# Expert outputs scattered by token inside the expert loop and read back with plain loads; the gated unit without its products of resident weights

## The reference

```python
x = x + 0.5 * moe(layernorm(x))      # 8 experts, 2 a token, F=512, layer norms inside
x = x + gated_unit(layernorm(x))     # groups of 64, relu^2 scores, linear part
x = x + 0.5 * moe(layernorm(x))      # the same weights again
x = x + 0.5 * swiglu_moe(layernorm(x))
x = x + attention(layernorm(x))
x = x + 0.5 * swiglu_moe(layernorm(x))
```

```python
probs, idx = top_k(softmax(xt @ Wr + br), 2); probs = probs / probs.sum()
h = layernorm(relu(xt @ W1[e] + b1[e])) * g1[e] + be1[e]
y = layernorm(relu(h @ W2[e] + b2[e])) * g2[e] + be2[e]
out = sum over the two chosen e of probs[e] * y[e]
```

## Time and profile before

| | |
|---|---|
| median of three runs | 2130.17 us (2128.75 to 2130.4) |
| the profiled execution | 2112.62 us, span 2110.8 us |
| mean granted TensorE clock | 0.908 |
| busy: TensorE | 1813.6 us, 86% |
| busy: TensorE weight loads | 1379.7 us, 65% |
| busy: VectorE | 1239.8 us, 59% |
| busy: ScalarE | 689.7 us, 33% |
| busy: GpSimd | 584.9 us, 28% |

### The profile page before, as it was taken

How to read it: one execution, slowest core, us unless ns; L and a number is a source line. 1 busy time by engine, 2 the same in 40 slices (tenths; PEclk the granted TensorE clock), 3 DMA queues, 4 the chain that set the end, 5 groups by cost and what they waited for, 6 DMA issues and landing times.

```text
span 2110.8 us, 38449 instructions
## 1 busy us (share of the span) xinstructions
PE 1813.6 (86%) x10812; PEld 1379.7 (65%) x10813; DVE 1239.8 (59%) x4206; ACT 689.7 (33%) x1279; POOL 584.9 (28%) x946
## 2 busy tenths in 40 slices
PE   3758994899844699299999969999999998999998
PEld 2547992555533699289988955555555555988987
DVE  2555885555545588566666555665655652556654
ACT  0114551222200355122232214444444442232222
POOL 2652675566257366532211010000000000000000
PEclk9758996999855799699999969999999998999999
DMA  5111212000001121100000000000000000000001
GB/s 200 38 43 51 60 50 93 25 20 21 3 29 45 57 60 55 55 21 12 19 11 11 1 0 1 1 0 0 0 0 0 0 0 1 1 0 0 0 1 41
DMA packets 61796, 54.18 MB, mean 26 GB/s; under 512 B 8579, under 2 KB 55044, under 8 KB 61189
## 3 DMA queue, kind: packets, MB, share of 16 engines
q1 hardware_dynamic: 52070, 34.20, 5.3%
q0 software_dynamic: 8192, 16.79, 2.7%
q10 hardware_dynamic: 1440, 2.10, 0.3%
HBM read 31.56 MB, written 21.50 MB: 25 GB/s over the span
## 4 chain that ended last, share of the span: by engine, by line
PE 70%; POOL 10%; DVE 8%; issue 8%; DMA 2%; SPq 1%; POOLq 1%; ACT 1%; DVEq 1%; ACTq 0%
PE bk L1007 14%; PE bk L1664 10%; PE bk L582 6%; PE bk L990 5%; PE bk L992 5%; PE bk L991 5%; POOL xs L368 4%; PE bk L1652 3%; PE bk L575 3%; PE bk L1639 2%; PE bk L1590 2%; PE bk L564 2%; PE bk L565 2%; PE bk L566 2%; DMA sb_X<-x 1%
## 5 line engine op out<-in xcount | busy, mean ns | idle before, releaser
L1007 PEld LDWEIGHTS bk<-sb_wd,sb_sc 128*128 128x128 f32 (+1 forms) x2688 | 333.0, 192 | 23.2 <-DVE sb_X L1106 3.6
L1007 PE MATMUL bk<-sb_wd,sb_sc 128*128 128x128 f32 (+1 forms) x2688 | 336.7, 275 | 0.0
L1092 DVE TENSOR_TENSOR sb_sc<-sb_sb_,bk 128x512 f32<-128x512 f32 x224 | 152.2, 684 | 230.4 <-PE bk L992 220.2
L112 POOL TENSOR_TENSOR sb_ln_ve<-sb_ln_mv,sb_eps 128x2 f32<-128x2 f32 (+1 forms) x48 | 9.4, 195 | 998.9 <-DVE sb_ln_mv L104 998.9
L1046 ACT ACTIVATE sb_sb_<-bk 128x512 f32<-128x512 f32 x224 | 133.8, 598 | 444.8 <-PE bk L992 442.0
L1918 DVE TENSOR_REDUCE sb_sc<-bk 128x2 f32<-128x512 f32 x256 | 164.6, 688 | 157.0 <-PE bk L1639 153.0
L1664 PE MATMUL bk<-sb_sa,sb_sb_ 128*32 128x256 f32 x1024 | 249.1, 387 | 0.7 <-ACT sb_sc L1813 0.7
L1826 ACT ACTIVATE sb_sa<-bk 128x512 f32<-128x512 f32 x256 | 151.1, 597 | 185.0 <-PE bk L1652 184.9
L1106 DVE SCALAR_TENSOR_TENSOR sb_X<-bk,sb_gate,sb_X 128x128 f32 (+1 forms) x576 | 161.4, 342 | 4.2 <-PE bk L1007 1.8
L582 PE MATMUL bk<-sb_w2c,sb_sb_ 128*128 x1152 | 152.2, 275 | 0.0
L368 POOL DMA_INDIRECT xs<-sb_xn,sb_send_row x128 | 128.7, 1006 | 80.3 <-DVE sb_send_row L357 44.0
(11 more groups left out here) (284 smaller groups left out, 3427.4 us busy)
## 6 DMA issues: line engine op xcount, KB each, us to landing
sb_sc<-xs SPq DMA_DIRECT2D x144, 64.0 KB, 1.9
ys<-sb_sc SPq DMA_DIRECT2D x36, 256.0 KB, 2.3
xs<-sb_xn,sb_send_row POOLq DMA_INDIRECT x128, 2.2
out<-sb_X SPq DMA_DIRECT2D x1, 2048.0 KB, 8.7
sb_sa<-w SPq DMA_DIRECT2D x1, 1792.0 KB, 14.2
sb_sc<-w SPq DMA_DIRECT2D x1, 1792.0 KB, 17.5
sb_sa<-w_gu SPq DMA_DIRECT2D x1, 1760.0 KB, 6.8
xs<-sb_zeros SPq DMA_DIRECT2D x24, 64.0 KB, 1.6
```

The source lines that it names most:

```text
L1007: ins = pe.matmul(bank[:, j * P:(j + 1) * P], p.hT[0:m, c % HRING, j * P:(j + 1) * P], p.wd[0:m, q * D:(q + 1) * D], start=(c == FIRST[e] ...
L1092: dve.tensor_tensor(p.hT[0:m, c % HRING, :], p.sg[0:m, c % 2, :], p.bk[2 + c % 2][0:m, :], ALU.mult)\
```

## The change

Each row that is scattered into `xs` now carries two more numbers, its token and its first-chosen expert, so a slot knows where its result belongs. Empty rows come from an input (`empty_rows`) that carries numbers of unused places. VectorE works out the destination row of each slot (four small operations in `unit_x_low`). GpSimd scatters each finished unit into `y2`, ordered by token and choice, with four indirect DMAs (`moe_back`), and the next phase reads `y2` with plain loads from SyncE (`combine_sp`). The subtraction of the mean and the gain are one VectorE operation (`moe_c`), the output scale is applied by ScalarE (`moe_scale_act`), GpSimd only adds the bias, and both scales are one pair of GpSimd operations on 128x8 (`moe_scales`). The bias of the last two units is added by VectorE (`moe_last_dve`), and their scatters stand at the end of GpSimd's queue. The products L1244 are gone. The core of the diff:

```diff
@@ route_rows_dve
+    dve.tensor_copy(p.xn[:, par, :, D], p.token[:, tiles_g])
+    dve.tensor_copy(p.xn[:, par, :, D + 1], p.rt_i[:, :, 0])
@@ the combine
-def combine_pool(pool, p, g, taken, k):
-    pool.wait_ge(p.comb_idx.sem, p.comb_idx.at(g + 1))
-    pool.sem_inc(p.pool_passed.sem, 1)
-    for j in range(TG):
-        pool.indirect_dma_start(taken[k][:, j * D:(j + 1) * D], None, p.ys,
-                                bass.IndirectOffsetOnAxis(ap=p.take_row[:, k, j:j + 1], axis=0)).then_inc(p.got.sem, 16)
+def combine_load_sp(sp, p, g, taken):
+
+    sp.wait_ge(p.comb.sem, p.comb.at(TOP * TG * g))
     for k in range(TOP):
+        sp.dma_start(taken[k].rearrange("p (j d) -> p j d", d=D),
+                     p.y2[k * NTOK + g * W:k * NTOK + (g + 1) * W, :].rearrange("(j p) d -> p j d", p=P))\
+          .then_inc(p.got.sem, 16)
+
+def combine_sp(sp, p, taken):
     for par in range(2):
+        sp.wait_ge(p.ystored[par].sem, p.ystored[par].at(0))
+    for g in range(NG):
+        combine_load_sp(sp, p, g, taken)
@@ the expert stage, SyncE
-        sp.wait_ge(p.xt.sem, p.xt.at(k - 1))
+        sp.wait_ge(p.xld.sem, p.xld.at(k - 1))
...
-def tiles_store_sp(sp, p, k, par):
...
@@ the expert stage, ScalarE
+def moe_scale_act(act, p, k, par):
+
+    act.wait_ge(p.dve_c.sem, p.dve_c.at(NC * k + NC))
     for j in range(TG):
+        act.activation(p.yo[:, par, j, :], p.yo[:, par, j, :], ACT.Copy, scale=p.rs[:, 1 - par, TG + j:TG + j + 1])\
+           .then_inc(p.act_s.sem, 1)
+
+
+def moe_act_unit(act, p, k, par, ahead=True, last=False, behind=True):
+    for j in range(TG):
+        if j == TG - 1 and behind:
+            moe_scale_act(act, p, k - 3, 1 - par)
@@ the expert stage, VectorE
 def unit_x_low(dve, p, k, par):
     dve.wait_ge(p.xhd.sem, p.xhd.at(k + 1))
+    tiles_k = bass.ds(k * TG, TG)
+    token, first = p.slots[:, par, :, D], p.slots[:, par, :, D + 1]
+    dve.tensor_tensor(p.slot_k[:, 0], first, p.t_exw[:, bass.ds(k * TG + 1, TG)], ALU.not_equal).then_inc(p.slot_of.sem, 1)
+    dve.scalar_tensor_tensor(out=p.slot_k[:, 1], in0=first, scalar=0.0, in1=p.iota72[:, tiles_k],
+                             op0=ALU.is_lt, op1=ALU.mult).then_inc(p.slot_of.sem, 1)
...
@@ moe_b
-    dve.wait_ge(p.pl_r.sem, p.pl_r.at(NR * k + 2))
-    if not first:
-        dve.wait_ge(p.pl_u.sem, p.pl_u.at(NU * (k - 1)))
+    dve.wait_ge(p.pl_s.sem, p.pl_s.at(2 * k + 2))
@@ moe_c
-        dve.tensor_scalar(y[:, j, :], y[:, j, :], p.mv2[:, par, j, 0:1], p.rs2[:, par, j:j + 1],
-                          ALU.subtract, ALU.mult).then_inc(p.dve_c.sem, 1)
+    if not first:
+        dve.wait_ge(p.pl_u.sem, p.pl_u.at(NU * (k - 1)))
+    dve.wait_ge(p.pl_s.sem, p.pl_s.at(2 * k + 4))
+    dve.sem_inc(p.dve_passed.sem, 1)
     for j in range(TG):
+        dve.scalar_tensor_tensor(out=p.yo[:, par, j, :], in0=p.y[:, par, j, :], scalar=p.mv[:, 1 - par, TG + j, 0:1],
+                                 in1=p.g2b[:, bass.ds(expert_of(word, j + 1) * D, D)],
+                                 op0=ALU.subtract, op1=ALU.mult).then_inc(p.dve_c.sem, 1)
@@ the expert stage, GpSimd
+def moe_back(pool, p, k, par, done, n):
+
+    pool.wait_ge(p.slot_of.sem, p.slot_of.at(4 * k + 4))
+    pool.sem_inc(p.pool_passed.sem, 1)
+    pool.tensor_copy(p.slot_send[:, par, :], p.slot_row[:, bass.ds(k * TG, TG)]).then_inc(p.slot_to.sem, 1)
+    pool.wait_ge(p.slot_to.sem, p.slot_to.at(k + 1))
+    pool.wait_ge(done.sem, done.at(n))
+    pool.sem_inc(p.pool_passed.sem, 1)
+    for j in range(TG):
+        pool.indirect_dma_start(p.y2, bass.IndirectOffsetOnAxis(ap=p.slot_send[:, par, j:j + 1], axis=0),
+                                p.yb[:, par, j, :], None).then_inc(p.ystored[par].sem, 16)
 
 
 def moe_pool_unit(pool, p, k, par, first=False):
-    moe_r(pool, p, k, par)
-    moe_u(pool, p, k - 2, par, p.pool_passed, p.pl_u, first)
-    moe_g(pool, p, k - 1, 1 - par)
+    moe_u(pool, p, k - 3, 1 - par, first)
+    moe_back(pool, p, k - 3, 1 - par, p.pl_u, NU * (k - 2))
+    moe_scales(pool, p, k, par)
...
@@ its end
+    moe_u(pool, p, UNITS - 3, 1)
+    moe_scales(pool, p, UNITS, 0, hidden=False)
+    moe_back(pool, p, UNITS - 3, 1, p.pl_u, NU * (UNITS - 2))
+    for n, k in enumerate((UNITS - 2, UNITS - 1)):
+        pool.wait_ge(p.ystored[n].sem, p.ystored[n].at(32 * (k - n)))
+        moe_back(pool, p, k, n, p.dve_u, NU * (n + 1))
@@ the gated unit
-def ga_warm_pe(pe, p, n):
-
-    for _ in range(n):
-        pe.matmul(p.bk[5][:, 0:S], p.w1h[:, 0:P], p.w1h[:, 0:S], start=True, stop=True)
...
 def ga_pool(pool, p):
-    combine_begin_pool(pool, p, p.ga_taken)
     ln_scale(pool, p, 0, NB2, True)
     ln_scale(pool, p, 1, NB2, True)
...
+    ln_scale(pool, p, 2, NB2, True)
+    with pool.Fori(0, B - 3) as b:
+        ln_scale(pool, p, b + 3, NB2, True)
+        ga_out_pool(pool, p, b)
```

More of the change, by code:

```diff
@@ L653, in moe_experts_act @@
         moe_relu(act, p, 0, j)
-    with act.Fori(0, UNITS // 2 - 1) as i:
+    for k in range(4):
+        moe_act_unit(act, p, k, k % 2, behind=k == 3)
+    with act.Fori(2, UNITS // 2 - 1) as i:
         moe_act_unit(act, p, 2 * i, 0)
@@ L709, in moe_dve_unit @@
         unit_x_low(dve, p, k + 2, par)
-    moe_c(dve, p, k - 2, par)
+    moe_c(dve, p, k - 2, par, first)
     moe_b(dve, p, k - 1, 1 - par)
@@ L2210, in _ @@
                         load(sp, dst, io[src], p.dma_at.sem)
+                if n and p.phases[n - 1] == "moe":
+                    combine_sp(sp, p, p.ga_taken if phase == "gau" else p.sw_taken)
                 if phase == "moe":
```

237 lines of the change are left out of this document (93 added, 144 removed).

## The result

The changed kernel takes 2233.26 us (median of 4 runs, 2231.48 to 2236.71) beside 2129.46 us for the kernel before; the ratio is 1.0496, 95% interval 1.0472 to 1.0519. The forecast was slower, 2188 us, 2146 to 2226: right in its direction, 45 us short, and outside its range. The profiled execution of the changed kernel spans 2231.7 us. The one of before spans 2110.8 and was 17.6 us faster than the median of its kernel, so differences between the two profiles add up to 121, not 104.

The account below looks back on a forecast made before the run. GpSimd's 9.72 us pass was taken to bound the expert loops: 2112.6 profiled + 71.4 loops + 2 routing - 6.4 handovers - 7.9 gated unit = 2171.7; with 17.6 to the median 2189, stated as 2188, range 2146 to 2226.

Parts of the forecast that it names:

- GpSimd's queue would be over the unit's 8.55 us: Expert loop: one GpSimd pass, with scatters, takes 9.72 us against 8.55 a unit, and all engines follow; +35.7 a mixture.
- Both at nothing: GpSimd's pass hides them: Expert loop: added work a unit, 0.8 us on VectorE and about 1.1 on ScalarE, costs no time behind GpSimd's pass.
- The drain at the stage's end: Expert stage's end: the 5.52 us from GpSimd's end to the next phase stays as it is, possibly down to 0.
- The clock term of the gated unit: Gated unit, products of resident weights removed: no gain from TensorE's freed time, and +8 us in the stretch's sum.
- Rival 4: Gated unit: the clock falls for good without the products, 4 to 5 us more an element; +70, 2258 us; chance 0.04.
- The gathers of the gated unit: Gated unit: without gathers, group 1's combine wait goes (-3.9) and elements take 12.0 us instead of 12.84 (-12).
- The handovers: Plain loads in place of gathers: 0 before the gated unit, -6.4 us behind the second mixture, with a 2 us landing.
- Rival 1: Expert loop: VectorE slows GpSimd's DMAs by 0.9 to 1.5 us a unit; +27 to +45, 2215 to 2233 us; chance 0.10.

Follow-up runs that it names:

- b_nowarm: The kernel before without its 158 products of resident weights in the gated unit, nothing else changed; ratio 1.0060 to the kernel before.
- a_warm: The changed kernel with the products of resident weights put back at their five places in the gated unit; ratio 1.0411 to the kernel before.

## Why the prediction missed

- **That GpSimd's queue would be over the unit's 8.55 us**: right, and each term of it to 0.15 us; own work 9.65 for 9.72, first add 204.30 for 203.9, the end behind the last add 22.2 for 22.0, the scatter 0.96 and 0.30 as in the earlier trace rows. This gave the direction.
- **"Both at nothing: GpSimd's pass hides them"**: this is the step that failed, for ScalarE above all. The 15 passes took 161.0 us (204.30 to 365.26) and not 145.8; 16.5 of them are twelve waits of GpSimd for ScalarE's scaling. I had given ScalarE 1.1 us more of work a unit (the four scalings take 1.26) and no wait of its own. In its place the runs showed that beside the scatters ScalarE starts up to 1.83 us late, 2.2 us a pass, and that its scaling stands between the held ReLU and the copy for which TensorE waits; GpSimd, with the longest queue, waits for that round. I had worked out queues, each for itself, and neither the round trip nor what the scatters do to a neighbour. It is +15.2 in the first mixture and +16.7 in the second (162.5 for the 15 passes), some 32 of the 45 us. VectorE, too, was taken with 0.8 more and a cover. Its four small operations cost 0.75, as sized, but without scatters it alone sets 10.06, because its two-input operation is half as long again beside GpSimd's adds (0.54 for 0.35 an instruction), and I had no term for that.
- **The drain at the stage's end**: 6.82 for 5.52, +1.3.
- **The clock term of the gated unit**: +8 taken, with 0 to +20 as its ends; b_nowarm and a_warm put it at 13 and 17 to 18. The mechanism was named and mis-sized: not four more elements with a low stretch but nearly all. Rival 4, the clock gone for good, did not come: the mean clock is 0.74 and not 0.50, so half of each element is still at the high level, and an element is 13.4 us instead of 12.3, not 4 to 5 more. The Trainium skill, "TensorE: Matmul & The Clock Gate", Part 1, has the clock low unless activity releases it; the trace agrees in direction (0.94 with the products and 0.75 without, from 430 to 600 us).
- **The gathers of the gated unit**: -12 and -3.9 predicted (15.9 together); a_warm against before gives -15.6. Right.
- **The handovers**: -6.4 predicted, -4.3 measured; the first combine starts 4.0 us after its two loads were issued, with 2 assumed.
- **Rival 1, scatters slowed by VectorE** (0.10) pointed at contention and had the victim the wrong way round; that its price, 2215 to 2233, ends at the measured time is luck.
- **The range**: its upper end took half of rival 1 and the clock's bound, but had nothing for a wait added to a queue that was already full. The direction was right for the reason given, GpSimd's longer queue; the time came from waits that were not in the sum.
